# A gelu perceptron and the attention over memory that follows it, in two blocks or in one

## The reference

```python
h = layernorm(y) * g + b                     # 1792 x 256
x = x + y + gelu(h @ W_ff1.T) @ W_ff2.T      # hidden width 1024
h = layernorm(x)
q = h @ Wq + bq                              # 16 heads of 16
k = concat(ctx @ Wk + bk, 4 * m_k)           # 375 + 64 keys
v = concat(ctx @ Wv + bv, 8 * m_v)
x = x + softmax(mask(q @ k.T)) @ v @ Wo + bo
```

## Time and profile before

| | us |
|---|---|
| median of 3 runs | 1696.06 (1693.14 to 1696.42) |
| profiled execution, its own time | 1704.48 |
| span of it, first to last instruction | 1702.7 |
| PE busy in the span | 1549.3 (91%) |
| DVE busy | 910.1 (53%) |
| ACT busy | 807.5 (47%) |
| POOL busy | 464.3 (27%) |

### The profile page before, as it was taken

The page is one execution under the profiler, slowest core; times in us unless marked ns, Lnnn a source line. Parts: engine busy times, 40 slices in busy tenths (PEclk is TensorE's granted clock), DMA queues, the critical chain, the costliest instruction groups (busy, mean ns, idle before and its releaser), DMA issues. The chain is left out here.

```text
span 1702.7 us, 34539 instructions
## 1 busy us (share of the span) xinstructions
PE 1549.3 (91%) x13478; PEld 1007.4 (59%) x13478; DVE 910.1 (53%) x1883; ACT 807.5 (47%) x1581; POOL 464.3 (27%) x416
## 2 busy tenths in 40 slices
PE   8899999799799999999799999999787899899965
PEld 3345544455356666656565899999344566556642
DVE  4578777421555565555242211111274898677758
ACT  4356555333144544455432222222255788476766
POOL 0132332321100000000028300000721777455622
PEclk9999999899999999999789999999999899799988
DMA  7000000010200000000043699997379534000001
GB/s 260 1 1 1 2 1 1 26 30 1 86 20 17 15 20 20 20 11 2 13 160 131 222 329 324 327 325 260 90 185 219 133 78 107 13 12 13 2 1 44
DMA packets 147796, 149.89 MB, mean 88 GB/s; under 512 B 69890, under 2 KB 134850, under 8 KB 147634
## 3 DMA queue, kind: packets, MB, share of 16 engines
q1 hardware_dynamic: 144562, 140.34, 26.8%
q0 software_dynamic: 3072, 7.34, 1.4%
HBM read 120.14 MB, written 27.53 MB: 87 GB/s over the span
## 5 line engine op out<-in xcount | busy, mean ns | idle before, releaser
L2567 DVE TENSOR_TENSOR masked<-masked 128x512 f32<-128x512 f32 x70 | 49.8, 711 | 200.9 <-ACT masked L2469 200.9
L958 DVE CUSTOM_DVE_ANT_0 x_unused<-psum,masked 112x439 f32<-112x439 f32 x256 | 141.9, 611 | 18.8 <-PE psum L781 18.0
L896 ACT ACTIVATE x_probs<-psum,key_mask 125x448 f32<-125x448 f32 x192 | 105.9, 634 | 76.1 <-PE psum L801 76.1
L2410 PEld LDWEIGHTS psum<-mix_xb,mix_up 128*128 128x128 f32 x1120 | 130.6, 192 | 2.1 <-issue 0.4
L2410 PE MATMUL psum<-mix_xb,mix_up 128*128 128x128 f32 x1120 | 130.7, 275 | 0.0
L2420 PE MATMUL psum<-mix_down,masked 128*128 128x256 f32 x560 | 127.0, 380 | 0.1
L2080 POOL TENSOR_TENSOR fold_part<-fold_part,a_rden 112x896 f32<-112x896 f32 x32 | 53.8, 1699 | 227.3 <-DVE a_rden L1942 227.3
L1481 PE MATMUL psum<-fold_full,hT 128*112 128x512 f32 x256 | 113.7, 597 | 1.8 <-DVE fold_part L1894 1.8
L2420 PEld LDWEIGHTS psum<-mix_down,masked 128*128 128x128 f32 x560 | 103.6, 190 | 13.3 <-DVE masked L2567 0.4
L1032 POOL TENSOR_TENSOR x_mixT<-x_mixT,x_rden 128x448 f32<-128x448 f32 x16 | 18.2, 1137 | 313.6 <-ACT x_rden L902 313.6
L781 PE MATMUL psum<-x_kT,x_qz 32*112 32x439 f32 x512 | 87.1, 580 | 3.2 <-DVE x_kT L943 3.2
(11 more groups left out here) (343 smaller groups left out, 3299.3 us busy)
## 6 DMA issues: line engine op xcount, KB each, us to landing
mix_up<-in_moe_up SPq DMA_DIRECT2D x35, 1024.0 KB
mix_down<-in_moe_down SPq DMA_DIRECT2D x35, 1024.0 KB
offset_rows<-join_rows SPq DMA_DIRECT2D x16, 784.0 KB, 5.8
hrow<-offset_rows SPq DMA_DIRECT2D x16, 784.0 KB, 5.4
x_ctx<-in_ctxT SPq DMA_DIRECT2D x16, 375.0 KB, 3.1
slots_x<-masked SPq DMA_DIRECT2D x1, 4480.0 KB, 21.2
mix_rows<-slots_x SPq DMA_DIRECT2D x35, 128.0 KB, 3.3
slots_y<-mix_result SPq DMA_DIRECT2D x35, 128.0 KB, 3.4
```

Of the source, the lines that this page charges most:

```text
L896: nc.scalar.activation(probs[0:rows, 4 * (c % 2) + r], psum[0:rows, bank("tile", n, 4 * c + r), 0:G].rearrange("p (k t) -> p k t", k=4), A ...
L958: nc.vector.tensor_tensor_reduce(unused[:, at], psum[0:T, at, 0:KEYS], masked[0:T, n * KEYS:(n + 1) * KEYS], -1.0, -3.0 * NEG, ALU.add, AL ...
L2410: mm = nc.tensor.matmul(psum[:, 2 * u + half, m * BLOCK:(m + 1) * BLOCK], e_up[:, w, c, (half * H4 + m) * P:(half * H4 + m + 1) * P], xb[: ...
L2567: nc.vector.tensor_tensor(e_hidden[:, u, half * H4:(half + 1) * H4], e_relu[:, half], e_relu[:, half], ALU.mult).then_inc(hidden_ready.sem, 1)
```

## The change

The two blocks become one. `gelu_perceptron` no longer opens a block; it returns five functions, one for each engine, and the block of `memory_attention` calls them ahead of its own work (`front["pe"](pe, first_operands)` and so on).

- **PE**: the queries of group 0 and the keys of batch 0 (8 products) are made in banks 0 to 3 instead of 4 to 7, after the sixth of the eight rows of down products of the last group (k == 5). The second quad of scores of batch 0 waits for the perceptron's last addition, since that reads banks 4 and 5.
- **DVE**: in the last group the key mask and all constants of the memory (`prepare_memory`) come before the norm's centring; after the norm's scaling DVE takes the queries and odd keys (`take_first`), and only then waits for the down products and adds them.
- **ACT**: takes the even keys after the last norm; a second load of its table is gone.
- **POOL**: fills `negmax` and `v` after the sums of the second group, clears retired semaphores once instead of twice, and waits for the last addition at its end.
- **SP**: loads the first three contexts right behind the weights, and waits for the last down product before it loads the next stage's weights.
- Buffers: `qz` lies in `yT`, `probs` in `hidden`, `v`, `unused`, `rden`, `qmax` and `key_bias` in buffers of the stage before. All counters of the attention are started ahead of the perceptron.

```diff
 def perceptron_sp(sp, first_contexts):
+    load_flags(sp)
+    next_weights.load(sp)
+    first_contexts()
+    sp.wait_ge(*hidden_read.after(At(LAST), M8 - 1))
 def perceptron_pe(pe, first_operands):
...
                 mm.then_inc(hidden_read.sem, 1)
                 if k == 5:
                     norm.variance(pe, other, 7)
+                    if g == LAST:
+                        pe.wait_ge(*act_done.after(n, M8 - 1))
+                        first_operands()
 def perceptron_dve(dve, prepare_memory, take_first):
...
+            if g == LAST:
+                mask_keys(dve, g)
+                prepare_memory()
             norm.centre(dve, other, 6)
             norm.scale(dve, other)
-            mask_keys(dve, g)
+            if g < LAST:
+                mask_keys(dve, g)
+            else:
+                dve.wait_ge(*joined.after(n))
+                take_first()
             dve.wait_ge(*hidden_read.after(n, M8 - 1))
             dve.wait_ge(*joined.after(n))
             nc.vector.tensor_tensor(accT[:, :, t], accT[:, :, t], psum[:, 4:4 + C, 0:G], ALU.add).then_inc(added.sem, 1)
 def perceptron_pool(pool, fill):
...
             if g:
                 pool.wait_ge(*added.after(At(g - 1)))
                 beside.behind.sum_halves(pool, g - 1)
                 beside.behind.sum_squares(pool, g - 1)
+            if g == 1:
+                fill()
+        pool.wait_ge(*added.after(At(LAST)))
...
 def scores(n, quad):
...
+                    if bank(*use) == 4 and n == 0 and quad == 1:
+                        pe.wait_ge(*front["added"])
                     wait_bank_read(pe, *use)
...
-            w.wait(pe)
-            queries(0, 0, 4)
-            queries(0, 1, 5)
-            keys(0, 0, 6)
-            keys(0, 1, 7)
+            def first_operands():
+                w.wait(pe)
+                queries(0, 0, 0)
+                queries(0, 1, 1)
+                keys(0, 0, 2)
+                keys(0, 1, 3)
+
+            front["pe"](pe, first_operands)
             pe.wait_ge(memory_ready.sem, 13)
...
-            nc.scalar.preload_act_table_set("natural_log_exp_and_others")
+            front["act"](act)
...
-            take_keys(0, 0, 6)
-            take_keys(0, 1, 7)
+            take_keys(0, 0, 2)
+            take_keys(0, 1, 3)
...
+            def prepare_memory():
+                w.wait(dve)
+                (the same 13 instructions as before, lines 984 to 994)
+
+            def take_first():
+                take_queries(0, 0, 0)
+                take_queries(0, 1, 1)
+                dve.wait_ge(memory_ready.sem, 4)
+                take_odd_keys(0, 0, 2)
+                take_odd_keys(0, 1, 3)
+
+            front["dve"](dve, prepare_memory, take_first)
...
             normed.start(pool)
-            Scope.clear_retired(pool)
-            filled.inc(nc.gpsimd.memset(negmax[:], 0.0))
-            filled.inc(nc.gpsimd.memset(v[:], 1.0))
+            front["pool"](pool, fill)
             beside.pool_sum(pool, 0)
```

More of the change, by code:

```diff
@@ L568, with gelu_perceptron @@
 UPS_AHEAD = 4
-def gelu_perceptron(nc, psum, w, hT, accT, yT, beside, next_weights, load_flags, mask_keys, ups_ahead):
+def gelu_perceptron(nc, s, psum, w, hT, accT, yT, beside, next_weights, load_flags, mask_keys, ups_ahead):
     up, down = w.at["up"], w.at["down"]
[L577 to L592, removed]
-            w.wait(pe)
[L594 to L630, removed]
-                nc.scalar.preload_act_table_set("natural_log_exp_and_others")
[L632 to L641, removed]
-                mask_keys(dve, g)
-                dve.wait_ge(*hidden_read.after(n, M8 - 1))
-                dve.wait_ge(*joined.after(n))
[L645 to L649, removed]
-            Scope.clear_retired(pool)
[L651 to L659, removed]
@@ new lines, in perceptron_act @@
+    def perceptron_act(act):
+        act_done.start(act)
+        for g in range(GROUPS):
+            n = At(g)
+            if g:
+                nc.scalar.preload_act_table(ACT.Gelu)
+            for m in range(M8):
+                if g == 0 and m < UPS_AHEAD:
+                    act.wait_ge(ups_ahead, m + 1)
+                else:
+                    act.wait_ge(*up_ready.after(n, m))
+                act.wait_ge(*hidden_read.after(n - 1, m))
+                nc.scalar.activation(hidden[:, m], psum[:, m % 4, 0:G], ACT.Gelu).then_inc(act_done.sem, 1)
+            norm, other = (beside.before, GROUPS - 1) if g == 0 else (beside.behind, g - 1)
+            norm.square(act, other)
+            nc.scalar.preload_act_table_set("natural_log_exp_and_others")
+            norm.invert_root(act, other, 7)
@@ new lines, in perceptron_dve @@
+    def perceptron_dve(dve, prepare_memory, take_first):
+        added.start(dve)
+        for g in range(GROUPS):
+            n, t = At(g), slice(g * G, (g + 1) * G)
+            norm, other = (beside.before, GROUPS - 1) if g == 0 else (beside.behind, g - 1)
+            if g == LAST:
+                mask_keys(dve, g)
+                prepare_memory()
+            norm.centre(dve, other, 6)
+            norm.scale(dve, other)
+            if g < LAST:
+                mask_keys(dve, g)
+            else:
+                dve.wait_ge(*joined.after(n))
+                take_first()
+            dve.wait_ge(*hidden_read.after(n, M8 - 1))
+            dve.wait_ge(*joined.after(n))
+            nc.vector.tensor_tensor(accT[:, :, t], accT[:, :, t], psum[:, 4:4 + C, 0:G], ALU.add).then_inc(added.sem, 1)
@@ new lines, in perceptron_pool @@
+    def perceptron_pool(pool, fill):
+        joined.start(pool)
+        Scope.clear_retired(pool)
+        beside.before.sum_halves(pool, GROUPS - 1)
+        beside.before.sum_squares(pool, GROUPS - 1)
+        for g in range(GROUPS):
+            t = slice(g * G, (g + 1) * G)
+            nc.gpsimd.tensor_tensor(accT[:, :, t], accT[:, :, t], yT[:, :, t], ALU.add).then_inc(joined.sem, 1)
+            if g:
+                pool.wait_ge(*added.after(At(g - 1)))
+                beside.behind.sum_halves(pool, g - 1)
+                beside.behind.sum_squares(pool, g - 1)
+            if g == 1:
+                fill()
+        pool.wait_ge(*added.after(At(LAST)))
@@ L662 @@
+    return {"sp": perceptron_sp, "pe": perceptron_pe, "act": perceptron_act, "dve": perceptron_dve, "pool": perceptron_pool, "hidden": hidden, "added": added.after(At(LAST))}
 CHUNK = 125
@@ L681, with memory_attention @@
 USE_AT = {use: at for at, use in enumerate(BANK_USES)}
-def memory_attention(nc, psum, const, w, hT, accT, ctxT, beside, next_weights):
+def memory_attention(nc, psum, const, w, hT, accT, ctxT, beside, next_weights, front, yT, fold_part, fold_full):
     ident = const["ident"]
@@ L738, in _, with first_contexts @@
         def _(sp):
-            for n in range(3):
-                ctx_load(sp, n)
+            def first_contexts():
+                for n in range(3):
+                    ctx_load(sp, n)
+            front["sp"](sp, first_contexts)
             next_weights.load(sp)
@@ L1021, in _, with fill @@
         def _(pool):
+            def fill():
+                filled.inc(nc.gpsimd.memset(negmax[:], 0.0))
+                filled.inc(nc.gpsimd.memset(v[:], 1.0))
             normed.start(pool)
-            Scope.clear_retired(pool)
-            filled.inc(nc.gpsimd.memset(negmax[:], 0.0))
-            filled.inc(nc.gpsimd.memset(v[:], 1.0))
+            front["pool"](pool, fill)
             beside.pool_sum(pool, 0)
```

78 lines of the change are left out of this document (51 added, 27 removed).

## The result

| | before | changed |
|---|---|---|
| median of 6 runs, us | 1695.62 (1693.14 to 1703.47) | 1687.71 (1682.25 to 1688.25) |
| ratio to before, 95% interval | | 0.9944 (0.9926 to 0.9962) |
| profiled execution, us | 1704.48 | 1687.89 |
| span of it, us | 1702.7 | 1686.1 |

What follows compares the result with a forecast made beforehand. PE, busy 91% of the span, was taken as the bound, its idle time at the perceptron-attention boundary as winnable. 9.4 us gained less 0.8 lost gave 8.6, off the 1696.06 us median: 1687.5 us, range 1683.5 to 1692.0.

Steps and rivals of the forecast that it cites:

- First products: Last group's down products: the queries and keys moved ahead of the last two rows cost 5.5 us of PE.
- The takings hidden: Perceptron's end: DVE and ACT take queries and keys 1.7 us before the last down products end.
- The chance of 0.06 against it: Rival at the perceptron's end: takings not hidden, a wait delays addition and maxima; 1692.7 us or more, chance 0.06.
- Addition and first maximum: Seam into attention: addition follows the last down by 0.38 us, first maximum at 440.45 instead of 448.35, 7.9 us gained.
- First batch at full clock: Attention's batch 0: keys take 1.50 us, not 2.87, and first values start 9.4 us earlier.
- What it costs at the start: Perceptron's start: eight attention counters ahead on PE delay the first product by 0.8 us, between 0.5 and 1.3.
- another fall: Rival in batch 0 or later: one more clock fall costs 2.4 or 3.3 us, 1689.9 to 1690.8 us, chance 0.12.
- Edits at nothing: POOL's fill, DVE's constants and mask, SP's contexts, ACT's table load: none moves the sum unless its cover is gone.
- The sum: Whole kernel: 9.4 - 0.8 = 8.6 us gained, taken off the median of 1696.06 us, giving 1687.5 us.
- The rule weighed: Pauses behind the change: the clock gate's own clock decides which are punished, and all now fall 8.6 us earlier.

Runs made afterwards that it cites:

- products behind: Changed kernel with the queries and keys behind all of the last down products instead of ahead of the last two rows; 1691.58 us, ratio 0.9971.
- constants behind: Changed kernel with DVE making the memory's constants after taking the queries, as before the change; 1702.72 us on the second chip, ratio 0.9974.
- one block only: Changed kernel with queries and keys after all last down products and the memory's constants after the queries on DVE; 1696.67 us, ratio 1.0003.
- next keys: Changed kernel with PE's attention counters after the first up products and second batch's keys made within the last downs; 1694.91 us on second chip, ratio 0.9932.
- late counters: Changed kernel with PE's eight attention counters started behind the first group's up products; 1682.97 us, ratio 0.9937; second chip 1697.89 us, 0.9945.

## Why the prediction was right, and where it was off

The time came out at 1687.71 us where 1687.5 were forecast, and that is closer than the steps deserve: by the trace the stage won 6.7 us and not 8.6, and the scatter of the medians made up for most of what was missing (the forecast was taken off a median of 1696.06 us for before, which more runs put at 1695.62). That the number was hit so closely is luck. The mechanism of the gain was right; the price at the perceptron's start was not.

- *First products, 5.5 us within the downs.* Right: 436.05 to 441.58 is 5.53 us.
- *The takings hidden, with 1.7 us of room.* Right: 1.6 us. The chance of 0.06 against it was not needed; "products behind" and "constants behind" show that the room is real, since each uses it up and pays 1.6 and 0.8 us.
- *Addition and first maximum.* The maximum was put at 6.97 us behind 433.48; from the variance that is 10.9 us, and it is 10.49.
- *First batch at full clock, 9.4 us at the first values.* Measured 9.76. The clock stayed at 1.00, and the keys took 1.53 us.
- *What it costs at the start: 0.8 us, between 0.5 and 1.3.* This step failed: 2.9 us. It had two errors. First, it let PE's counters run beside ACT's gelu and took the longer way. But the first gelu also waits for `hidden_read`, the tenth of PE's counters, so they stand in one chain: counters, gelu, product. (From the gelu to the product are 0.69 us before, 336.34 to 337.03, and after, 340.38 to 341.07.) The wait stood in the code (`hidden_read.after(n - 1, m)`), and the line of ACT above says so: in the trace of before the gelu at 336.34 was released by a counter on PE's queue, and I had read only PE's line of the pair. (ACT's own counters, which the prediction put at 0.8 us, took 0.3, six of them from 338.8 to 339.1, and ended ahead of PE's.) That gives 1.24 us (2.37 - 1.13), still within the step's own 0.5 to 1.3 us; the measured 2.9 us are not. Second, it priced a pause of PE by its length only. It asked of the seam what the clock would do, and not of the place where it made a pause longer: from 1.78 to 2.99 us, behind which the clock was low and the up products cost 1.7 us more. The rival "another fall" had the right mechanism with a chance of 0.12 and looked for it behind the seam, in batch 0 or later.
- *Edits at nothing.* Right as a whole: fill, contexts, mask and table load leave no wait of their own on the chain, and the attention's later part is unchanged to 0.1 us. The shift at the first values was thus carried to the end, as forecast; it is 6.8 us from the meeting on (119.91 to 113.09), and 4.0 by the span's own time (455.81 to 451.79), since this profile reached the meeting 2.8 us later.
- *The sum.* 9.76 - 2.94 - 0.1 = 6.7 us by the trace in place of 8.6. The medians of the first runs differ by 7.9 us and the ratio on the second chip gives 6.7; both intervals hold 6.7 as well as 8.6, so the times alone would not have found the error.
- *The rule weighed.* The forecast took from it that a shift moves which short pauses are punished. In the changed kernel it moved none: its falls behind the first values lie at the same 34.5 and 292 us as before. In other kernels the same work met a fall or didn't. From 9.4 to 13.4 us behind the first values the old kernel had

```profile
465.20:469.20 4.00, 3.70 (x40) 2.31 (x42) 2.07 (x8) 2.21 (x5) 1.13 (x1) 1.00 0.00 0
```

and the same kernel with eight more counters, 9.4 to 13.4 us behind its first values (460.61),

```profile
470.00:474.00 4.00, 3.70 (x34) 2.86 (x34) 2.07 (x8) 1.64 (x4) 1.13 (x1) 0.65 0.00 0
```

with the same work and the same pauses ahead of it from the first values on. Such a fall is there too with the products behind, with one block only and with the next keys, and in none of the others. A fall 200 us behind the first values is there with the late counters (both times), with the products behind and with the next keys, and in none of the others. The pause of 2.99 to 3.03 us at the perceptron's start was followed by a low clock in all six profiles that had it, on two chips, and that of 1.78 to 1.88 us in none of the four that had it; but the low clock lasted longer in one of the six ("constants behind"), where the work up to there is the same as in four of the others. So the pause just ahead doesn't decide alone. That fits what the Trainium skill states in "TensorE: Matmul & The Clock Gate", section "What's actually happening", the rule that the prediction weighed: the gate is checked on a clock of its own, which doesn't start with the kernel. But no run here sets the phase by itself: the kernels differ in what lies ahead of the first values, and where one kernel was profiled twice (the changed one, and the late counters) it had its falls behind the first values at the same places both times, on two chips. That the falls follow the phase, which is where a pause lies on a clock of the gate's own, remains an inference.

## What to carry to other kernels

When work is merged in front of a stage, count what its preamble issues, counters too, and follow which engine waits for the last of them: here eight counters took 1.3 us in a chain of three engines and 1.7 us more through the clock, together three tenths of what the merge with its new order won. Removing a meeting of engines is worth little while the work behind it stays in one chain; moving the operand products, and with them the constants that their taking waits for, in front of work that needs nothing of them was worth more than the meeting with the early fill (5.6 us against 4.1 at the first values), since it covers their taking and keeps TensorE busy. Ask of every pause of TensorE that a change makes longer what the clock may do behind it, and not only of the one that it removes. Compare stages by their own marks, since the whole span carried 9.9 us of differences (16.6 - 6.7) that were not the change's.

## What the runs showed of the hardware that I had not expected

- Starting a counter costs PE's queue about 0.14 us each (ten from 338.9 to 340.2 in the changed profile), though the profile gives its own duration as 51 ns.
- A pause of TensorE that grew from 1.8 to 3.0 us brought the granted clock from 1.00 to 0.66 in the 5 us behind it, in five of six profiles and to 0.50 in the sixth, and cost 1.7 us, or 3.0 in that one; at the seam a low clock stood behind pauses of 3.13 us (0.65 in 437 to 440, before) and 3.24 us (0.50 in 443.4 to 446.4, one block only).
- The length of the pause alone doesn't tell: at the seam with the products behind the clock was low behind 1.66 us (0.64 in 442 to 446), while at the perceptron's start it stayed at 1.00 behind 1.78 to 1.88 us.
- Short falls of the clock come and go at one and the same work: with 0.23 us of pause ahead of it, 28 records of tiles took 2.55 us in the kernel with the next keys, and 1.66 us behind the same pause with the late counters.
- One stage far from the change, the join of the mixture's results, took 104.6 to 106.3 us in five profiles (the changed kernel and four more on the first study chip), 115.0 to 115.8 in the four of the second chip, and 113.2 in the profile of before; why is open.
